# A rotary layer's opening moved into the last block of the routed experts before it

## The reference, cut to what matters

```
x = x + routed_experts(LN(x))          # 64 experts, 8 chosen per row, and a shared one
h = LN(x)
for l in range(4):                      # the rotary layers
    xn = LN(h) * ln1_w[l] + ln1_b[l]
    q, k, v = xn @ Wq.T + bq, xn @ Wk.T + bk, xn @ Wv.T + bv        # 16 heads of 8
    scores = (q k^T + rel_shift((q + u) r^T)) / sqrt(8), causal
    h = h + softmax(scores) v @ Wo.T + bo
    h = h + gelu(LN2(h) @ W1.T + b1) @ W2.T + b2
```

## Time and profile before

| | |
|---|---|
| median of three executions | 6044.86 us |
| profiled execution | 6047.05 us, its span 6045.3 us |
| TensorE busy | 5537.8 us (92%) |
| VectorE, ScalarE, GpSimd busy | 4178.4 (69%), 2810.2 (46%), 2251.0 us (37%) |
| routed experts, first to last `hidden` | some 580 to 1994 us |
| first rotary block starts | 2004.6 us |

### The profile page before, as it was taken

The page is one execution under the profiler, slowest core; times in us unless marked ns, Lnnn a source line. Parts: engine busy times, 40 slices in busy tenths (PEclk is TensorE's granted clock), DMA queues, the critical chain, the costliest instruction groups (busy, mean ns, idle before and its releaser), DMA issues. The chain is left out here.

```text
span 6045.3 us, 119428 instructions
## 1 busy us (share of the span) xinstructions
PE 5537.8 (92%) x37453; PEld 3434.4 (57%) x37453; DVE 4178.4 (69%) x9588; ACT 2810.2 (46%) x4608; POOL 2251.0 (37%) x3170
## 2 busy tenths in 40 slices
PE   7997999999999699999999999999997879886777
PEld 5664444444444377647775677567754456644564
DVE  6785666666666588648874788478856866578764
ACT  3554222222222255545555455555555655544354
POOL 5662000000000366526653566256633532253312
PEclk9998999999999799999999999999998989997799
DMA  4332322232323455425551565155510000000002
GB/s 128 106 106 99 98 95 96 98 97 96 97 96 98 116 157 158 112 70 144 158 143 40 143 158 158 29 146 158 158 44 5 0 7 0 1 4 0 1 1 64
DMA packets 526333, 527.07 MB, mean 87 GB/s; under 512 B 55698, under 2 KB 436705, under 8 KB 503780
## 3 DMA queue, kind: packets, MB, share of 16 engines
q1 hardware_dynamic: 517684, 517.90, 30.6%
q10 hardware_dynamic: 8320, 5.25, 0.4%
HBM read 337.88 MB, written 185.07 MB: 87 GB/s over the span
## 5 line engine op out<-in xcount | busy, mean ns | idle before, releaser
L987 DVE TENSOR_REDUCE a_mx<-a_unit 128x2 f32<-128x512 f32 (+1 forms) x1536 | 1034.4, 687 | 305.8 <-PE a_unit L1359 300.6
L1176 ACT ACTIVATE a_prob<-a_slot 128x1536 f32<-128x1536 f32 x512 | 742.7, 1451 | 553.3 <-PE a_slot L1382 469.9
L2009 ACT ACTIVATE f_silu<-f_pG 128x512 f32<-128x512 f32 x528 | 314.8, 598 | 937.2 <-PE f_pG L2084 923.2
L1357 PE MATMUL a_unit<-a_sk,a_sq 96*128 96x128 bf16 (+1 forms) x4096 | 596.2, 249 | 19.8 <-DVE a_mx L987 10.4
L1951 DVE TENSOR_TENSOR f_gated<-f_spread,f_silu 128x512 f32<-128x512 f32 x512 | 354.5, 692 | 353.0 <-ACT f_silu L2009 308.9
L2061 PE MATMUL f_pO<-f_hidden,f_wd 128*128 128x512 f32 x1056 | 546.4, 599 | 13.1 <-DVE f_hidden L1953 12.5
L60 POOL TENSOR_SCALAR f_veps<-f_moments 128x4 f32<-128x4 f32 (+1 forms) x112 | 25.3, 226 | 1421.8 <-DVE f_moments L1838 1021.3
L2084 PE MATMUL f_pG<-f_xnT,f_wg 128*128 128x512 f32 x1056 | 542.8, 596 | 0.0
L2088 PE MATMUL f_pU<-f_xnT,f_wu 128*128 128x512 f32 x1056 | 540.5, 593 | 0.0
L1359 PE MATMUL a_unit<-a_maskq,identb 128*128 128x256 bf16 (+1 forms) x1536 | 480.6, 313 | 1.8 <-issue 1.8
L920 POOL TENSOR_SCALAR_AFFINE_SELECT a_prob<-a_prob 128x512 f32<-128x512 f32 x384 | 244.6, 637 | 500.9 <-ACT a_prob L1176 488.9
(11 more groups left out here) (470 smaller groups left out, 12199.4 us busy)
## 6 DMA issues: line engine op xcount, KB each, us to landing
f_spread<-f_scratch SPq DMA_DIRECT2D x1024, 128.0 KB, 2.9
a_sq<-a_qscratch SPq DMA_DIRECT2D x128, 768.0 KB, 5.7
a_sk<-a_kscratch SPq DMA_DIRECT2D x160, 384.0 KB, 6.6
a_qscratch<-a_parts SPq DMA_DIRECT2D x288, 192.0 KB, 2.2
a_qscratch<-a_parts SPq DMA_DIRECT2D x288, 128.0 KB, 2.2
a_kscratch<-a_parts SPq DMA_DIRECT2D x160, 192.0 KB, 2.2
a_kscratch<-a_parts SPq DMA_DIRECT2D x160, 128.0 KB, 2.2
a_qscratch<-a_parts SPq DMA_DIRECT2D x288, 64.0 KB, 1.8
```

Source lines behind the costliest of these rows:

```text
L987: v.tensor_reduce(dst, src, op=ALU.max, axis=AX.X, negate=True).then_inc(red_done, 1)
L1176: act.activation(prob[gr % 2][:, :], slot[:, :], ACT.Exp, scale=SCALE).then_inc(exp_done, 1)
L1357: pe.matmul(bank[:, at * wide:(at + 1) * wide], q, sk[b][0:KM, gr * GH + h, 0:wide], start=(at == 0), stop=False)
L2009: act.activation(silu[c % 2][:, :], pG[c % 2][:, :], ACT.Silu).then_inc(silu_done, 1)
```

## The change

The five functions of a rotary layer's opening move out of `rotary_layers` into a class `RotaryOpening`, which holds their tiles and semaphores and is made before the experts' stage. `routed_experts` gets it as `following` and calls it between the steps of its last block only. `rotary_layers` has no `start_layer` any more; it uses the same functions in its steps and in `EARLY`. The constants of `RotaryKept` are loaded one buffer at a time in the new block, each with its own semaphore, ahead of the stack of the same buffer; `output_bias` stands before the first step. The rotary layers' later work is the same.

```diff
@@ routed_experts @@
+    AHEAD = {n: 6 * (n + 5) for n in range(-5, 0)}
+        def at(c, delay, first=-4):
+            return [n for n in AHEAD if n >= first and AHEAD[n] + delay == c]
@@ sync @@
+                following.first_loads(sp)
...
+                        if last(n):
+                            for m in at(c, 13):
+                                following.write_parts(sp, m, m // 4, m % 4)
+                    if last(n):
+                        following.write_parts(sp, -1, -1, 3)
@@ gpsimd @@
+                    if last(n):
+                        following.add_biases(g)
+                        following.scale_of(g, chain, -5)
+                        following.scale_of(g, chain, -4)
...
+                    if last(n):
+                        for m in range(-4, 0):
+                            following.gather(g, chain, m, m // 4, m % 4)
+                            following.split(g, chain, m, m % 4)
+                            if m < -1:
+                                following.scale_of(g, chain, m + 1)
@@ vector @@
+                        if last(n):
+                            for m in at(c, 0, -5):
+                                v.drain()
+                                following.take_stats(v, chain, m)
+                            for m in at(c, 3, -5):
+                                following.norm(v, m)
+                            for m in at(c, 5):
+                                if m == -4:
+                                    v.wait_ge(following.turn_in, 16)
+                                    v.wait_ge(following.b12_done, 1)
+                                following.rotate(v, m)
@@ scalar @@
+                            for m in at(c, 0):
+                                if m == -4:
+                                    act.wait_ge(following.w_qk, following.W_QK)
+                                following.turned(act, m, m % 4)
+                            for m in at(c, 3):
+                                following.projected(act, m)
@@ tensor @@
+                            for q in at(c, 0):
+                                following.turn_rows(pe, q)
+                            for q in at(c, 2):
+                                if q == -4:
+                                    pe.wait_ge(following.w_qk, following.W_QK)
+                                following.project(pe, q, q % 4)
+                            for q in at(c, 4):
+                                following.project_turned(pe, q, q % 4)
@@ rotary_layers, sync @@
-                attn_weights(0)
-                kept.load(sp, core)
+                kept.masks(sp, core)
+                for b in range(4):
+                    kept.rows(sp, core, b)
+                    if b < 3:
+                        read_stacks(b - 3, -1, b + 1)
+                    if b == 0:
+                        out_weights(0)
                 feed_weights(0)
-                early_steps()
@@ vector @@
-                start_layer()
+                output_bias()
                 open_steps(step)
@@ tensor, maxima @@
+                        if u == 0 and isinstance(n, int) and m < 4:
+                            pe.wait_ge(kept.rows_in[m], 32)
@@ tensor @@
-                start_layer()
+                pe.wait_ge(kept.masks_in, 32)
```

More of the change, by code:

```diff
@@ new lines, with __init__, masks, rows @@
+class RotaryKept:
+    def __init__(self, nc, stack, tag):
+        k = Held(nc, stack, tag)
+        self.held = k
+        self.sk = [k.sb(f"sk{b}", [98, HEADS, SEQ], BF16) for b in range(4)]
+        self.vaug = [k.sb(f"vaug{b}", [P, QT, HEADS, 32]) for b in range(2)]
+        self.ones3 = k.sb("ones3", [P, P], BF16)
+        self.maskq, self.maskk = k.sb("maskq", [P, P], BF16), k.sb("maskk", [P, P], BF16)
+        self.masks_in, self.filled, self.zeroed = k.sem("masks_in filled zeroed")
+        self.rows_in = [k.sem(f"rows_in{b}") for b in range(4)]
+    def masks(self, sp, core):
+        sp.dma_start(self.maskq[:, :], core["maskq"]).then_inc(self.masks_in, 16)
+        sp.dma_start(self.maskk[:, :], core["maskk"]).then_inc(self.masks_in, 16)
+    def rows(self, sp, core, b):
+        sp.dma_start(self.sk[b][0:48, :, :], core["kturn"].unsqueeze(1).broadcast_to((48, HEADS, SEQ))
+                     ).then_inc(self.rows_in[b], 16)
+        sp.dma_start(self.sk[b][96:98, :, :], core["ones2"]).then_inc(self.rows_in[b], 16)
+    def fill(self, g):
+        for b in range(2):
+            g.memset(self.vaug[b][:, :, :, :], 0.0).then_inc(self.zeroed, 1)
+        g.memset(self.ones3[:, :], 1.0).then_inc(self.zeroed, 1)
+        g.wait_ge(self.zeroed, 3)
+        for b in range(2):
+            pairs = self.vaug[b][:, :, :, :].rearrange("p t (r f j) e -> p (t r) f j e", f=2, j=GH)
+            for f in range(2):
+                ins = g.memset(pairs[:, :, f, :, 16 * f + HD:16 * f + HD + 1], 1.0)
+        ins.then_inc(self.filled, 1)
@@ L711, in rotary_layers @@
+def rotary_layers(nc, core, tag, store, eps, w, wf, layers, kept, o):
     NS = 3
@@ L726, in rotary_layers @@
         bo3 = k.sb("bo3", [P, D], BF16); warm = k.sb("warm", [P, 1])
[L727 to L732, removed]
+        mhalf, xnT, wq = o.mhalf, o.xnT, o.wq
         sq = [k.sb(f"sq{b}", [KS, HEADS, SEQ], BF16) for b in range(4)]
@@ L1498, in step @@
                     maxima(11)
-                def start_layer():
-                    pe.wait_ge(w_qk, W_QK)
-                    for n in range(-4, 0):
-                        turn_rows(n)
-                        project(n, n % 4)
-                        project_turned(n, n % 4)
-                    pe.wait_ge(kept.loaded, kept.loads)
                 def feed(following):
@@ L1534, in _ @@
                 feed(False)
-        for x in f.sems:
+        for x in f.sems + o.held.sems + o.once_only.sems:
             nc.gpsimd.sem_clear(x)
@@ L1762, in routed_experts, with last @@
         W_IN, ROUTER_IN = 16 * 6, 16 * 3
+        def last(n):
+            return once(n, BLOCKS - 1)
+        def at(c, delay, first=-4):
+            return [n for n in AHEAD if n >= first and AHEAD[n] + delay == c]
         def pairs(eng, step):
```

385 lines of the change are left out of this document (191 added, 194 removed).

## The result

| | before | after |
|---|---|---|
| first comparison, six executions each | 6044.41 us (6033.14 to 6055.24) | 6021.35 us (6008.89 to 6024.51), ratio 0.9956, 95% interval 0.9945 to 0.9968 |
| second comparison, nine and five | 6046.65 us (6037.2 to 6052.39) | 6016.5 us (6012.32 to 6019.76), ratio 0.9952, 0.9938 to 0.9966 |
| profiled execution | 6047.05 us, span 6045.3 | 6008.89 us, span 6007.2 |

The kernel is faster by 27 to 29 us by the ratios; 28.8 were forecast. The profiled execution of after is at the lower edge of its kernel, so the 38.1 us between the two spans are not all the change's.

What follows compares the result with a forecast made beforehand. The path was taken as last experts' block on TensorE, then constants, GpSimd's chain and sequence 0's stack. Boundary 41.7, less TensorE 8.0, lock 4.5, semaphores 0.4, gave 28.8 us: median 6016.0 us, range 6006 to 6026.

Steps and rivals of the forecast that it cites:

- the lock: Experts' last block: GpSimd passes reading SBUF hold up VectorE's `gated`, stalling TensorE; 4.5 us lost (0 to 8).
- the boundary: From experts' last block into the rotary block: preparation gone, first maximum earlier, less the maxima's return trip; net gain 41.7 us.
- First maximum: Rotary block's start: stack of sequence 0 lands, then `output_bias`; first maximum at 2018.7 instead of 2061.65, 42.9 us earlier.
- Return trip: First maxima's trip by ScalarE's queue, beside SyncE's queue that is never empty then: scores later, 1.2 us charged (0 to 3).
- TensorE's own instructions: Experts' last block, TensorE full: moved matmuls and transposes paid in full, 2.0 us per sequence, 8.0 us (7.8 to 9).
- Rival A: Experts' last block: `gated` is not held up, or the slack takes it; gain 33.3 us, 6011.6; chance 0.22.
- Spreads, ScalarE, the last writes, loads at the stage's head: Experts' stage: moved writes delaying spreads, added ScalarE reads, last sequence's writes and six early loads all hidden; 0 us.
- Five more semaphores: Clearing them at the end costs 0.4 us.
- rival C: TensorE's clock stays at 0.50 into the rotary main steps, 11 us lost per step; slower, 6071; chance 0.03.
- B: Rotary opening bound by SyncE's queue: late stack, unhidden bias, return trip 3 us late; 6021.7; chance with D 0.22.
- D: Experts' last block: GpSimd's chain so stretched that norms wait and last writes end after the block; 6024; chance 0.06.
- the signs: Expected in the trace: first maximum 14 us after block start, experts' last step 12.5 us later, TensorE waiting behind `hidden`.

Runs made afterwards that it cites:

- second pair of profiles: Kernel before and changed kernel, both word for word, profiled again: sums 199.4 and 171.6 us; the changed one timed at 6016.5 us, ratio 0.9952.
- return_trip_in_order: Changed kernel, but sequence 3's rows and stack and the feed weights wait on SyncE for the first maxima, stack behind feed weights; 6009.24 us, ratio 0.9944.
- gpsimd_writes_only: Changed kernel, but GpSimd only fills tiles where it added, split and subtracted (results not the layer's); experts' last block 93.47 us.
- return_trip_and_busy: Changed kernel with sequence 3's loads and feed weights held for the first maxima, stack ahead of feed weights, plus six unread TensorE matmuls before the masks; layers 2365.4 us.
- busy_until_maxima: As return_trip_in_order, with eleven unread f32 matmuls on TensorE before the masks and the output bias between the two open steps; 6017.18 us, ratio 0.9951.
- opening_back: Changed kernel with the opening back in the rotary block, in the old load order; constants keep their own semaphores; last block to first output projection 182.8 us.
- bias_after_open: Changed kernel with the first rotary layer's output bias made after the two opening steps instead of ahead; last block to first output projection 171.6 us.

## Why the prediction was right, step by step

Faster, and by the size forecast: 28.8 us against 27.8 to 30.5 in the sums and 27 to 29 by the ratios. The forecast median, 6016.0, is 5.4 below the first and 0.5 below the second. Two terms inside were off, with opposite signs, and that is luck: with the measured terms the sum is 41.8 - 2.6 - 7.8 - 0.8 - 0.1 = 30.5 us; the lock was 3.7 us cheaper than put in, the boundary gained 2.5 us less.

- **First maximum, 42.9 us earlier.** 41.8 (66.1 to 24.4 us after the experts' last `oT`). Stack 0 landed 12.0 us after the block's start, not 11.2, and the bias began 0.8 us later still, when the last of `out_weights` was in; its 2.4 us were right. It fell inside the bounds 2016 to 2022.
- **Return trip, 1.2 us (0 to 3).** The mis-sized half of the boundary: it cost 2.6 us. 7.8 us from write to read made the scores 1.76 us later against the maxima (22.3 for 20.6), and with the clock's fall behind the hole step 0 was 0.88 us longer (29.7 for 28.8); in the second pair of profiles these are 3.4 and 2.2. Net boundary 39.1 (36.4 in the second pair) for 41.7. The prediction looked at the read alone (6.6 us in the kernel before); in after the read took 2.0 us and the write before it came late, and the clock's part was not in the term. The Trainium skill (DMA: Bandwidth & Descriptors, Queues, rings and completion order) states that a completion is counted only behind earlier writes of its DMA engine, whatever their queue, from which the prediction had "nearer to 2 us than 0". The trace bears this out in part only: 4.2 of the 6.4 us that the write was longer in after than in return_trip_in_order passed before its first packet, 2.2 behind it. What holds the packets back is not shown.
- **TensorE's own instructions, 8.0.** 7.8 (gpsimd_writes_only against before).
- **The lock, 4.5 (0 to 8).** The term that failed in size: 0.8. It happened as laid out, `gated` up to 2.10 us beside the passes of 1.64, and was gone where GpSimd only writes, in line with the Trainium skill (SBUF — State Buffer, Who interferes with whom), which states that a VectorE instruction with two SBUF inputs contends with a GpSimd one that reads SBUF and not with one that only writes it. But "0.7 us is free" counted only the slack of a plain step. The opening's own matmuls, paid for in the term before, stand in TensorE's order behind the later of the two and cover the 0.7 us put in for it; and seven `gated` were late, not three for each of four sequences. Rival A's second half, "or the slack takes it", is what happened.
- **Spreads, ScalarE, the last writes, loads at the stage's head: 0.** The last block grew by 8.6 us, the two terms above, and no `gated` in it waited for a `spread`; the last write had landed at 1999.6, the block's end was at 2002.2.
- **Five more semaphores, 0.4.** 0.1: from the last `h_store` to the next stage's first load 5.92 us for 5.83.
- **Clock (rival C).** It was 1.00 for good 41.4 us after the block's start, in main step 0. C did not come; its cause did, for 3 us of that step. **B** had one third right, the late return trip; stack and bias were on the forecast's side. **D**: the last writes were out before the block's end.
- Of the signs: the first maximum 14 us after the start was 15.3; the last block 12.5 us longer was 8.6; TensorE stalled behind `hidden` in three of the four sequences, 0.3 us each instead of 1.1.

That 6008.89 was profiled and 6018.2 forecast for the profiled execution is for the most part the 8.2 us in which the two differ ahead of the experts' stage, in code that was not changed.

## What to carry to other kernels

Before work is moved to hide a wait, ask only for what the next instruction needs: with the opening left where it was, that alone gave 16.6 to 18.4 of the 29 us, part of it through an early clock, at no cost to the block before. Count slack on a full engine with the moved work in its queue: what is added there can also be cover. And behind a removed wait look for the next small transfer on another queue: a 16 KB write was 6.4 us longer behind loads that nobody needed yet; holding them back gave 3.0 and 4.8 us at the first output projection, taking the bias away from ahead of the maxima nothing.

## What was not expected of the hardware

- A DMA write of 16 KB on ScalarE's queue was counted after 1.4 us with SyncE's queue empty and after 7.8 with the constant rows, the feed weights and a stack issued ahead of it on SyncE's; its first packet came after 0.8 and after 5.0 us.
- The clock went to 1.00 3.8 and 4.1 us after the f32 matmuls of return_trip_and_busy and busy_until_maxima began, and 18 to 24 us after the bf16 maxima began in the others but opening_back, where it rose 2.5 us after (f32 matmuls of the preparation stand right ahead of them there). It went back to 0.50 at holes of 1.7 (gpsimd_writes_only) to 5.5 us (bias_after_open). Behind a hole of some 2.5 us at the opening TensorE worked 3 to 7 us at half clock.
- Unchanged stages differ by 7 to 11 us from one execution to the next (the last stage 1450.9 to 1461.8 us), while the experts' last block repeats within 0.03 us in eight kernels with the same moved work (in return_trip_in_order and busy_until_maxima it was 0.3 us shorter, with one stall of the lock less): a gain of 10 us needs marks inside the trace, or many rounds.
